# Local attention with its value product in banks of its own, and clipped attention issued two tiles at a time

## The chip, the cores and the metric

The kernel runs on one core of a Trainium2 chip. The metric is the device time of one execution in microseconds (us). Three timed runs of the kernel before took 2329.82, 2330.53 and 2332.7 us; their median is 2330.53 us. One further execution was profiled: it took 2336.06 us, of which the trace covers a span of 2334.3 us. All durations below are from that one.

## What is computed

The program is a chain of eight stages on 2048 tokens of width 128 (four attention layers and four feed-forward blocks), each with its own residual and normalisation. Two of them are touched.

The local stage has two layers. In each, queries and keys are normalised per head, turned by a rotary table, and a block of 64 queries attends to its own 64 keys and the 64 before:

```python
sim = einsum('bhwid,bhwjd->bhwij', bq, bk)       # 8 heads, 64 queries against 128 keys
mask = (i < j) | (i > j + WINDOW) | (j == -1)
sim = where(mask, -finfo.max, sim)
out = einsum('bhwij,bhwjd->bhwid', softmax(sim), bv)
x = x + out @ wo                                  # then layer norm, w1, a * gelu(g), w2, residual
```

The clipped stage is full attention over 512 tokens with 16 heads of 64, and relative positions clipped to 16 steps either way:

```python
sim = q @ k.T * scale + einsum('btd,tsd->bts', q, rel_k_table[idx]) * scale
attn = softmax(sim)
out = attn @ v + einsum('bts,tsd->btd', attn, rel_v_table[idx])
return out @ Wo.T + bo
```

## The kernel before, in words

Every stage is a class with a written list of steps (`order`), and one method for each engine (`on_tensor`, `on_vector`, `on_scalar`, `on_gpsimd`, `on_sync`). Each engine walks the same list and takes the steps that are its own, so the list sets the order on each engine. Nothing overtakes on an engine. Steps wait on each other by semaphores (`w.wait_ge`). Between stages, the last steps of one (`tail`) are dealt out among the first steps of the next (`head`).

PSUM has eight banks of 128x512 fp32. `Turns` deals banks to the steps named in its table: strictly in turn over the list, so with k banks a step gets the bank of the step k places before it among those steps. `freed` returns the semaphore that the new step must wait for, which is the one given by the step that empties the bank: for a projection `lin` that is `s_square`, since ScalarE squares the projection out of the bank after VectorE has read it.

**Local stage** (span about 207 to 640 us). 32 steps n (16 tiles of 128 tokens, two layers). Step n of the list works at several tiles at once, with p = n + 5: scores of tile n, projections `lin` of tile p for queries and keys (two matmuls of 128x128 by 512 columns, L1558), VectorE's rotary products on them (L1663 to L1665), ScalarE's squares (`square`, L1761), the transposes of two finished outputs (`ot`, L1602, emptied at L1788) and of the exponentials (`flip`, two of them, L1585, emptied at L1784), the value projection `v` of tile n + 2 (L1558 again, emptied at L1768), the transposes of queries and keys (`turnq`, `turnk`, L1564, emptied at L1776 and L1684), the exponential (L1779), the output product `out` (L1607), and the value product `av` of tile n - 1 (L1596; VectorE divides it at L1699 and L1702). TensorE's order in a step is: scores, lin, lin, ot, flip, v, flip, turnq, turnk, out, av. Steps of the feed-forward block (L1614 to L1632) are put in every four steps, between the second `flip` and `turnq` or at the end of the step.

Scores (L1573, the mask added by an identity matmul; L1578, the products, in quarters of 64x64) and `av` share banks 0 and 1, so the scores of n wait until VectorE has divided the `av` of n - 2 (`v_av`). The other nine bank users of a step (lin, lin, ot, flip, v, flip, turnq, turnk, out) take banks 2 to 7 in turn: six banks.

**Clipped stage** (about 1600 to 2220 us). 32 head pairs p (8 pairs in each of 4 batches), each of 4 tiles of 128 queries: 128 tiles n. A tile is: scores of two heads against 512 keys (L2323, banks 0 and 1 or 2 and 3), VectorE adds the relative part (L2405) and takes the maximum (L2408), ScalarE the exponential (L2488), eight transposes (L2330) through banks 4, 5 and 7 in turn, emptied by VectorE (L2414) and ScalarE (L2496), and the value product into bank 6 (L2345). GpSimd multiplies the band of near positions (L2534). Once for each head pair: the projections `q` and `k` (L2292), every second time `rel` (L2308), the sums of the band (`xsum`, `sums`: L2419, L2425), their transposes `wt` (L2352), and the matmul `close` (L2357) that ends the pair's bank 6. In some tiles there are value projections `vals` (L2288) and output products `wo` (L2362).

SyncE issues all transfers of that stage in list order from one queue: `lay` (L2551) stores the table of relative scores to memory, `skew` (L2555) loads it back at a slant, `band` (L2562) stores a tile's band, `gather` (L2567) loads its diagonal, `send` (L2572) stores one row of `wt`, and `rep` (L2577) loads it back to 64 partitions. Their waits are in `on_sync`. In the list before, `send` of a head pair stands in its fourth tile, then come `gather` in the next first tile and `rep` behind it, and `lay` stands in the second tile.

Of the kernel before, what the change touches and what calls it, by code (L numbers as in the profile page):

```python
# [41 lines left out]
def _tables():  # L42
    bf = np.dtype(mybir.dt.np(BF))
    f = np.float32
    c = {}
# [42 lines left out]
    b["loc"] = neg((x > i + 64) | (x < i))  # L88
    b["loc0"] = neg((x > i + 64) | (x < i) | ((p < 64) & (x < 64)))

# [1312 lines left out]
class Local:  # L1403
# [7 lines left out]
    def __init__(self, C):  # L1411
# [27 lines left out]
        for r in range(4):  # L1439
# [6 lines left out]
        self.early = Turns(self.plan[:self.head], 4, {"lin": S["s_square"]})  # L1446
        many = {step: (2, 3, 4) for step in self.plan[last:]}
        many.update({step: range(5) for step in self.plan[late:last]})
        self.ring = Turns(self.plan[self.head:], 6, {"lin": S["s_square"], "v": S["s_v"], "turnq": S["s_turnq"], "turnk": S["v_turnk"],
                                         "flip": S["s_flip"], "ot": S["s_ot"], "out": S["v_out"],  # L1450
                                         "two": S["v_two"], "hg": S["s_hg"], "ha": S["v_ha"], "four": S["v_four"], "five": S["s_five"],
                                         "turnx": S["s_turnx"]}, lambda step: many.get(step, range(6)))
        self.past = ((S["v_lin"], 31, 1), (S["t_lin"], 31, 1), (S["g_sum"], 31), (S["v_sum"], 31), (S["s_square"], 31, 1),
                     (S["s_turnx"], 0), (S["v_four"], 4), self.ring.held[5])
        C.met, C.left = last - late, [(S["v_av"], 31), self.ring.held[0], self.ring.held[1]]

    def order(self):
# [12 lines left out]
        for n in range(5):  # L1470
# [3 lines left out]
            if n == 3:  # L1474
                plan.extend([("v", 0), ("even", 0), ("v", 1), ("even", 1)])
        plan.extend([("scale", 0), ("turnq", 0), ("turnk", 0)])
        for n in range(N + 2):
            p = n + 5
            if n < N:
                plan.append(("scores", n))  # L1480
            if n + 1 < N:
# [27 lines left out]
            if 0 <= n - 1 < N:  # L1509
                plan.append(("av", n - 1))  # L1510
            if n >= 2 and n % 4 == 1:
                L, at = n // 4 - 1, 2 * n
                work += [(at, L, [("roll", L)]), (at + 2, L, [("ln", L)]), (at + 4, L, [("two", L)]),
                         (at + 5, L, [("hg", L, 0)]), (at + 6, L, [("ha", L, 0), ("hg", L, 1)]), (at + 7, L, [("ha", L, 1), ("hg", L, 2)]),
                         (at + 8, L, [("ha", L, 2)]), (at + 9, L, [("four", L)])]
                if L < NB:
                    work.append((at + 10, L, [("five", L)]))
                else:
                    work += [(at + 9, L, [("add", L), ("fin", L - NB)]), (at + 11, L, [("turnx", L - NB)])]
# [17 lines left out]
    def bank(self, step):  # L1537
        for turns in (self.early, self.ring):
            if step in turns.slot:
                return self.C.bank[2 + turns.slot[step]]  # L1540

    def on_tensor(self, e, w, step):
# [23 lines left out]
        elif kind == "scores":  # L1566
            QT, mask = self.QT[n % 2], W["loc0" if q == 0 else "loc"].unsqueeze(1).broadcast_to((128, 4, 128))
            w.wait_ge(S["v_soft"], n - 1)
            w.wait_ge(S["v_av"], n - 2)
            w.wait_ge(S["s_turnq"], n)  # L1570
            w.wait_ge(S["v_turnk"], n)
            for r in range(2):
                e.matmul(C.bank[r].rearrange("p (c j) -> p c j", c=4), W["idb"], mask, start=True, stop=False)  # L1573
            for c in range(4):
# [12 lines left out]
        elif kind == "av":  # L1587
            PT = self.PT[n % 2]
            w.wait_ge(S["v_soft"], n + 1)
            w.wait_ge(S["v_av"], n - 1)  # L1590
# [3 lines left out]
            for h in range(8):  # L1594
                for k, V in enumerate((self.VE, self.VO)):
                    i = e.matmul(C.bank[h // 4][64 * k:64 * k + 64, 65 * (h % 4):65 * (h % 4) + 65],  # L1596
                                 PT[:, 4 * (h % 2) + h // 2, 64 * k:64 * k + 64], V[n % 4][:, h, :], start=True, stop=True)
# [41 lines left out]
    def on_vector(self, e, w, step):  # L1639
# [55 lines left out]
        elif kind == "av":  # L1695
            va, r = S["v_av"], self.NM[n % 2][:, 8:16].rearrange("p (a h) -> p a h", a=2)
            s = C.PS[:, 0:2, 0:260].rearrange("p a (h c) -> p a h c", c=65)
            w.wait_ge(S["t_av"], n)
# [464 lines left out]
class Clipped:  # L2163
# [57 lines left out]
    def order(self):  # L2221
        plan, N = [("init",), ("turn",), ("q", 0), ("k", 0), ("table",), ("rel", 0), ("qr", 0), ("lay", 0), ("skew", 0)], 128
        plan.extend(("vals", 0, k, hf) for k in range(NT) for hf in range(2))
        for n in range(N + 10):
            p, q = n // 4, n % 4
            ahead = n < N and p + 1 < 32
            if ahead and q == 1:
                plan.extend([("qr", p + 1), ("lay", p + 1)])
            if n < N:
                plan.append(("scores", n))  # L2230
            if ahead and q == 0:
                if p % 2:
                    plan.append(("rel", (p + 1) // 2))
                plan.append(("q", p + 1))
            m = n - 32 - 3
            if m >= 0 and m % 32 < 4 and n < N:
                plan.append(("vals", m // 32 + 1, m % 32, 0))
            if 0 <= n - 2 < N:
                plan.append(("backv", n - 2, 0))
                plan.append(("backv" if (n - 2) % 4 == 3 else "backs", n - 2, 1))  # L2240
            if m >= 0 and m % 32 < 4 and n < N:
                plan.append(("vals", m // 32 + 1, m % 32, 1))
            if ahead and q == 0:
                plan.append(("k", p + 1))
            if n < N:
                plan.append(("exp", n))
            if 0 <= n - 1 < N:
                plan.append(("band", n - 1))
            if ahead and q == 2:
                plan.append(("skew", p + 1))  # L2250
            if q == 0 and 0 <= p - 1 < 32:
                plan.append(("gather", p - 1))
            if q == 0 and 0 <= p - 1 < 32:
                plan.append(("xsum", p - 1))
            if q == 2 and 0 <= p - 1 < 32:
                plan.append(("sums", p - 1))
            if 0 <= n - 6 < N:
                plan.append(("av", n - 6))
            if q == 3 and 0 <= p - 1 < 32:
                plan.extend([("wt", p - 1), ("send", p - 1)])  # L2260
            if q == 0 and 0 <= p - 2 < 32:
                plan.append(("rep", p - 2))
            if q == 1 and 0 <= p - 2 < 32:
                plan.append(("close", p - 2))
            b, m = (n - 38) // 32, (n - 38) % 32
            if 0 <= b < NB:
                if m < 2:
                    plan.extend([("wo", b, 2 * m), ("wo", b, 2 * m + 1)])
                if m == 1:
                    plan.append(("fin", b))  # L2270
                if m == 3:
                    plan.append(("turnx", b))
        return plan

# [722 lines left out]
```

## Time and profile before

| | |
|---|---|
| median of three timed runs | 2330.53 us |
| profiled execution, its span | 2336.06 us, 2334.3 us |
| TensorE busy with matmuls | 2077.1 us, 89% of the span |
| VectorE busy | 1532.0 us, 66% |
| ScalarE busy | 1145.4 us, 49% |
| GpSimd busy | 746.8 us, 32% |
| mean TensorE clock granted | 0.954 of full speed |
| transfers | 198.86 MB, mean 85 GB/s |

How to read it: the profile names engines PE (TensorE matmul), PEld (its weight load), DVE (VectorE), ACT (ScalarE), POOL (GpSimd) and SP (SyncE, which only issues transfers here). An instruction's duration begins when it starts and includes the time until its result is there, so durations of instructions that follow each other overlap, and the pitch of a group is better read from the start of one group to the start of the next. "Idle before" is the time in which an engine had nothing running, and what released it.

### The profile page before, as it was taken

Reading aid. Unit: us, or ns where it says so; the run is one execution under the profiler, and the core shown is the slowest. Engines: PE = TensorE matmul, PEld = TensorE weight load, DVE = VectorE, ACT = ScalarE, POOL = GpSimd, SP = SyncE. Lnnn points to the kernel's source line nnn. Section 1 sums busy time; section 2 is a strip of 40 time slices with the busy share of each in tenths; the row PEclk is TensorE's granted clock in tenths of the full one; section 3 lists DMA queues with packets and bytes.
Section 4 is the critical chain, followed back from the end, with each engine's and each line's share of the span. In section 5 each row is a group of like instructions: output and inputs, shape, how many; then the busy total and the mean of one; then the engine's idle time right before and its main releaser. Section 6 shows DMA issues by size and latency. Waiting matters only on the chain.

```text
span 2334.3 us, 40576 instructions
## 1 busy us (share of the span) xinstructions
PE 2077.1 (89%) x15640; PEld 1221.0 (52%) x15640; DVE 1532.0 (66%) x3079; ACT 1145.4 (49%) x1854; POOL 746.8 (32%) x1057
## 2 busy tenths in 40 slices
PE   5886789998868988999998988998999999999988
PEld 2332456666644454545564443445665656656546
DVE  5675677778678777746557772106776777767663
ACT  2565456556613545573333565224654655646432
POOL 4544433333127846450011320003223232232133
PEclk7998899999979999999998999999999999999999
DMA  4430111111323524202002310002563554535252
GB/s 142 127 92 2 28 29 28 31 27 29 95 77 123 153 72 133 82 3 100 1 4 89 100 47 33 0 0 100 173 193 103 182 160 138 167 114 182 82 111 55
DMA packets 183975, 198.86 MB, mean 85 GB/s; under 512 B 55922, under 2 KB 152486, under 8 KB 179302
## 3 DMA queue, kind: packets, MB, share of 16 engines
q1 hardware_dynamic: 183782, 196.27, 28.3%
q8 instruction: 123, 2.02, 0.4%
q14 instruction: 70, 0.57, 0.1%
HBM read 93.53 MB, written 92.08 MB: 80 GB/s over the span
## 4 chain that ended last, share of the span: by engine, by line
PE 45%; DVE 5%; ACT 2%; issue 1%; POOL 1%; DMA 1%; SPq 0%; DVEq 0%; ACTq 0%; POOLq 0%
PE PS L2323 6%; PE PS L2345 5%; PE PS L2330 5%; PE PS L2093 5%; PE PS L1946 3%; PE PS L2292 2%; PE PS L1933 2%; PE PS L1936 2%; PE PS L2357 1%; PE PS L2672 1%; PE PS L2362 1%; PE PS L597 1%; PE PS L2660 1%; PE PS L2662 1%; PE PS L2288 1%
## 5 line engine op out<-in xcount | busy, mean ns | idle before, releaser
L1275 ACT ACTIVATE AR<-PS 128x1024 f32<-128x1024 f32 x160 | 162.5, 1023 | 121.3 <-PE PS L1024 120.4
L718 ACT ACTIVATE AR<-PS 128x1024 f32<-128x1024 f32 x160 | 162.7, 1024 | 93.5 <-PE PS L576 46.3
L2488 ACT ACTIVATE AR<-PS,AR 128x512 f32<-128x512 f32 x256 | 173.5, 685 | 64.0 <-DVE AR L2408 63.8
L1128 DVE TENSOR_REDUCE AR<-PS 128x2 f32<-128x768 f32 (+1 forms) x192 | 160.0, 865 | 50.1 <-PE PS L1004 27.2
L2534 POOL TENSOR_TENSOR RA<-AR,RA 128x288 f32<-128x288 f32 x128 | 89.0, 695 | 235.4 <-ACT AR L2488 231.9
L2408 DVE TENSOR_REDUCE AR<-PS 128x2 f32<-128x1024 f32 x128 | 156.8, 1225 | 11.1 <-DVE PS L2405 0.5
L2323 PE MATMUL PS<-AR 64*128 64x200 f32 (+2 forms) x1280 | 148.0, 359 | 3.6 <-ACT AR L2488 3.6
L2330 PE MATMUL PS<-CC,AR 128*128 128x128 f32 x1024 | 138.5, 279 | 0.0
L2330 PEld LDWEIGHTS PS<-CC,AR 128*128 128x128 f32 x1024 | 113.6, 142 | 41.4 <-issue 37.7
L2323 PEld LDWEIGHTS PS<-AR 64*128 64x128 f32 x1280 | 103.9, 188 | 58.5 <-issue 50.7
L1817 POOL TENSOR_TENSOR AR<-AR 128x1024 f32<-128x1024 f32 x32 | 75.4, 2356 | 183.7 <-DVE AR L1665 183.7
L2405 DVE TENSOR_TENSOR PS<-PS,AR 128x288 f32<-128x288 f32 (+1 forms) x128 | 61.7, 482 | 91.1 <-PE PS L2323 80.6
L2093 PE MATMUL PS<-AR,RA 128*128 128x512 f32 x256 | 110.2, 593 | 0.0
L1558 PE MATMUL PS<-RA,AR 128*128 128x512 f32 x192 | 101.0, 638 | 10.2 <-ACT AR L1743 7.0
L597 PE MATMUL PS<-AR 128*32 128x512 f32 (+3 forms) x1024 | 103.0, 479 | 2.8 <-POOL AR L781 1.9
L554 PE MATMUL PS<-AR 48*128 48x512 bf16 (+7 forms) x512 | 70.1, 336 | 33.6 <-ACT AR L718 13.1
L658 DVE TENSOR_REDUCE AR<-PS 128x2 f32<-128x1024 f32 x64 | 77.6, 1223 | 21.6 <-PE PS L559 20.8
L1037 PE MATMUL PS<-AR 128*32 128x128 f32 (+3 forms) x1024 | 85.8, 441 | 4.3 <-POOL AR L1355 3.8
L1352 POOL TENSOR_SCALAR_AFFINE_SELECT AR<-AR 128x512 f32<-128x512 f32 (+1 forms) x128 | 72.2, 566 | 50.5 <-ACT AR L1275 50.2
L2029 ACT ACTIVATE AR<-PS 128x512 f32<-128x512 f32 x64 | 37.8, 597 | 101.4 <-PE PS L1933 98.0
L660 DVE TENSOR_REDUCE AR<-PS 128x2 f32<-128x768 f32 x64 | 61.3, 958 | 39.0 <-PE PS L559 38.7
L2093 PEld LDWEIGHTS PS<-AR,RA 128*128 128x128 f32 x256 | 48.7, 190 | 60.6 <-issue 60.6
(367 smaller groups left out, 5003.3 us busy)
## 6 DMA issues: line engine op xcount, KB each, us to landing
ZD<-RC SPq DMA_DIRECT2D x32, 1152.0 KB
AR<-ZD SPq DMA_DIRECT2D x32, 640.0 KB
ZP<-AR SPq DMA_DIRECT2D x128, 160.0 KB, 2.9
SP<-AR SPq DMA_DIRECT2D x40, 384.0 KB, 2.6
AR<-SP SPq DMA_DIRECT2D x128, 96.0 KB
RA<-SP SPq DMA_DIRECT2D x32, 384.0 KB
SP<-AR SPq DMA_DIRECT2D x40, 256.0 KB, 2.9
RC<-RC SPq DMA_DIRECT2D x64, 130.0 KB
```

What stands on the lines that cost most here:

```text
L597: i = e.matmul(b6[32 * j:32 * j + 32, 128 * kb:512], self.VP[b % 2][:, 16 * kb + 4 * (k % 4) + j, :], self.PT[at % 6][:, r, a:a + wd], sta ...
L718: e.activation(self.PT[m % 6], C.PS[:, 2 * s:2 * s + 2, :], ACT.Exp).then_inc(S["s_turned"].sem, 1)
L1128: i = e.tensor_reduce(nm[:, :, 4 * up + q:4 * up + q + 1], src[:, :, a:a + wd], AX, ALU.max, negate=True)
L1275: e.activation(self.PT[m % 6], C.PS[:, 2 * s:2 * s + 2, :], ACT.Exp).then_inc(S["s_turned"].sem, 1)
L1558: e.matmul(o, self.HT[:, L % NB, 64 + 128 * q:192 + 128 * q], W["wqkv" + str(L // NB)][:, 512 * x:512 * x + 512], start=True, stop=True).t ...
L2093: m = e.matmul(ba, w4[:, k, 128 * c:128 * c + 128], src[:, k, :], start=k == 0, stop=k == 3)
L2323: i = e.matmul(C.bank[2 * (n % 2) + hh][:, lo:hi], self.QT[p % 2][h, 128 * q:128 * q + 128], src[p % 2][h, lo:hi], start=True, stop=True)
L2330: i = e.transpose(o[:, 128 * k:128 * k + 128], self.PP[n % 5][:, hh, 16 + 128 * k:144 + 128 * k], C.ident)
L2345: i = e.matmul(C.bank[6][64 * hh:64 * hh + 64, 128 * lo:128 * hi].rearrange("p (a c) -> p a c", a=hi - lo), V[:, k, 64 * h:64 * h + 64], p ...
L2408: e.tensor_reduce(self.NMX[n % 4], s, AX, ALU.max, negate=True).then_inc(S["v_scores"].sem, 1)
L2488: i = e.activation(self.PP[n % 5][:, hh, 16:528], C.bank[2 * (n % 2) + hh], ACT.Exp, bias=self.NMX[n % 4][:, hh:hh + 1], accum_out=self.DE ...
L2534: e.tensor_tensor(self.XM[:, 2 * q:2 * q + 2, :], self.PP[n % 5][:, :, 128 * q:128 * q + 144], W["edge"].unsqueeze(1).broadcast_to((128, 2 ...
```

## The change

In the local stage, `av` gets banks 2 and 3 for itself, the scores keep 0 and 1, and the other nine bank users of a step share banks 4 to 7: four banks in turn instead of six. `scores` of n + 1 stands right behind `av` of n - 1 in the list, ahead of the sums and of the feed-forward steps of that place, and no longer waits for `v_av`; `av` no longer waits for `v_soft`. The mask is added by four matmuls with a 64x64 identity instead of two with a 128x128 one. In the last steps three banks are dealt instead of five.

```diff
-        self.ring = Turns(self.plan[self.head:], 6, {"lin": S["s_square"], "v": S["s_v"], ...
+        self.ring = Turns(self.plan[self.head:], 4, {"lin": S["s_square"], "v": S["s_v"], ...
...
-                                         "turnx": S["s_turnx"]}, lambda step: many.get(step, range(6)))
+                                         "turnx": S["s_turnx"]}, lambda step: range(3 if step in few else 4))
...
+        plan.append(("scores", 0))
         for n in range(N + 2):
             p = n + 5
-            if n < N:
-                plan.append(("scores", n))
...
             if 0 <= n - 1 < N:
                 plan.append(("av", n - 1))
+            if n + 1 < N:
+                plan.append(("scores", n + 1))
...
             w.wait_ge(S["v_soft"], n - 1)
-            w.wait_ge(S["v_av"], n - 2)
...
-            for r in range(2):
-                e.matmul(C.bank[r].rearrange("p (c j) -> p c j", c=4), W["idb"], mask, start=True, stop=False)
+            for k in range(2):
+                for r in range(2):
+                    h = slice(64 * r, 64 * r + 64)
+                    mask = W["loc" if q or k else "loc0"][h].unsqueeze(1).broadcast_to((64, 4, 128))
+                    e.matmul(C.bank[r][64 * k:64 * k + 64, :].rearrange("p (c j) -> p c j", c=4), W["idb"][h, 64 * r:64 * r + 64],
+                             mask, start=True, stop=False)
...
             PT = self.PT[n % 2]
-            w.wait_ge(S["v_soft"], n + 1)
...
-                    i = e.matmul(C.bank[h // 4][64 * k:64 * k + 64, 65 * (h % 4):65 * (h % 4) + 65],
+                    i = e.matmul(C.bank[2 + h // 4][64 * k:64 * k + 64, 65 * (h % 4):65 * (h % 4) + 65],
```

In the clipped stage the list is written anew in pairs of tiles. What each step does is unchanged. The new body, for n = 0, 2, 4, ... with p = n // 4, and `first` for the first pair of a head pair:

```diff
+        for n in range(0, N + 12, 2):
+            p, first = n // 4, n % 4 == 0
+            ahead = n < N and p + 1 < 32
+            if first:
+                if 0 <= p - 2 < 32:
+                    plan.append(("rep", p - 2))
+                if ahead:
+                    plan.extend([("qr", p + 1), ("lay", p + 1)])
+                if 0 <= p - 1 < 32:
+                    plan.append(("gather", p - 1))
+            else:
+                if ahead:
+                    plan.append(("skew", p + 1))
+                if 0 <= p - 1 < 32:
+                    plan.append(("sums", p - 1))
             if n < N:
+                plan.extend([("scores", n), ("scores", n + 1)])
+            plan.extend(("av", m) for m in (n - 6, n - 5) if 0 <= m < N)
+            for m in (n, n + 1):
+                if m < N:
+                    plan.append(("exp", m))
+                if 0 <= m - 2 < N:
+                    plan.extend([("backv", m - 2, 0), ("backv" if (m - 2) % 4 == 3 else "backs", m - 2, 1)])
+                if m < N:
+                    plan.append(("band", m))
+            if first:
+                if ahead:
+                    plan.extend([("q", p + 1), ("k", p + 1)])
+                if 0 <= p - 1 < 32:
+                    plan.append(("xsum", p - 1))
+            else:
+                if ahead and p % 2 == 0 and p + 2 < 32:
+                    plan.append(("rel", p // 2 + 1))
+                if 0 <= p - 1 < 32:
+                    plan.extend([("wt", p - 1), ("send", p - 1)])
...
+            if first and 0 <= p - 2 < 32:
+                plan.append(("close", p - 2))
```

The value projections now stand four in a row at the end of a pair, the output products two in a row.

## Rows read from the trace of the kernel before

**Rows 1.** The page's costliest groups: busy, mean ns of one, idle before.

```profile
L2488 ACT ACTIVATE AR<-PS,AR 128x512 f32<-128x512 f32 x256 | 173.5, 685 | 64.0 <-DVE AR L2408 63.8
...
L2408 DVE TENSOR_REDUCE AR<-PS 128x2 f32<-128x1024 f32 x128 | 156.8, 1225 | 11.1 <-DVE PS L2405 0.5
```

**Rows 2.** TensorE in time order, one plain local step: start, busy, group [idle before].

```profile
300.74 0.60 PE L1573 MATMUL PS<-CB 128*128 128x512 bf16 x2 [1.04 <-DVE RC L1702]
...
301.28 1.10 PE L1578 MATMUL PS<-AR 64*64 64x128 f32 x32
...
302.31 1.99 PE L1558 MATMUL PS<-RA,AR 128*128 128x512 f32 x4
...
305.01 1.03 PE L1558 MATMUL PS<-RA,AR 128*128 128x512 f32 x2
...
305.87 0.60 PE L1585 MATMUL PS<-CC,AR 128*128 128x128 f32 x4
...
306.46 0.66 PE L1564 MATMUL PS<-CC,AR 128*128 128x128 f32 x4
...
307.44 0.66 PE L1564 MATMUL PS<-CC,AR 128*128 128x128 f32 x4 [0.32 <-ACT AR L1761]
...
308.92 1.15 PE L1596 MATMUL PS<-RC,AR 128*64 128x65 f32 x32
...
311.11 0.60 PE L1573 MATMUL PS<-CB 128*128 128x512 bf16 x2 [1.04 <-DVE RC L1702]
```

**Rows 3.** ScalarE in time order, the same step.

```profile
305.80 0.60 ACT L1761 ACTIVATE AR<-PS 128x512 f32<-128x512 f32 x1
306.28 0.62 ACT L1768 ACTIVATE RC<-PS 128x512 f32<-128x512 f32 x1
...
306.76 0.63 ACT L1761 ACTIVATE AR<-PS 128x512 f32<-128x512 f32 x1
```

**Rows 4.** TensorE, starts of the mask matmuls of two later local steps.

```profile
434.70 0.61 PE L1573 MATMUL PS<-CB 128*128 128x512 bf16 x2 [0.46 <-DVE RC L1702]
...
572.08 0.99 PE L1573 MATMUL PS<-CB 128*128 128x512 bf16 x2 [3.50 <-DVE RC L1702]
```

**Rows 5.** ScalarE, the first square in the local step with the normalisations.

```profile
428.83 0.60 ACT L1761 ACTIVATE AR<-PS 128x512 f32<-128x512 f32 x1 [1.19 <-DVE AR L1665]
```

**Rows 6.** TensorE, the key transposes of the same step.

```profile
430.75 0.65 PE L1564 MATMUL PS<-CC,AR 128*128 128x128 f32 x4 [0.61 <-ACT AR L1761]
```

**Rows 7.** Stretches: length, busy (count) of PE, PEld, DVE, ACT, POOL, clock, DMA.

```profile
381.00:383.00 2.00, 2.00 (x12) 1.78 (x12) 1.85 (x3) 1.97 (x3) 2.00 (x2) 0.51 0.57 130
```

**Rows 8.** TensorE in time order, clipped stage: one tile, and two matmuls that end head pairs.

```profile
1862.49 1.13 PE L2357 MATMUL PS<-AR,RA 128*128 128x512 f32 x2
1863.55 1.16 PE L2323 MATMUL PS<-AR 64*128 64x200 f32 x12
1864.63 1.09 PE L2330 MATMUL PS<-CC,AR 128*128 128x128 f32 x8
1865.65 1.08 PE L2345 MATMUL PS<-RA,AR 128*64 128x128 f32 x8
1866.67 1.14 PE L2323 MATMUL PS<-AR 64*128 64x256 f32 x8
...
1879.39 1.13 PE L2357 MATMUL PS<-AR,RA 128*128 128x512 f32 x2
```

**Rows 9.** SyncE's queue, clipped stage: start and duration of the issue.

```profile
1860.82 0.45 SPq L2551 DMA_DIRECT2D ZD<-RC  x1
...
1866.20 0.36 SPq L2555 DMA_DIRECT2D AR<-ZD  x1
```

**Rows 10.** Transfers issued in 1861.2 to 1862 (right behind a `lay`): KB, us to landing.

```profile
ZP<-AR SPq DMA_DIRECT2D x1, 160.0 KB, 4.9
```

**Rows 11.** Transfers issued in 1855.5 to 1857 (the queue otherwise empty).

```profile
ZP<-AR SPq DMA_DIRECT2D x1, 160.0 KB, 1.9
```

More of the change, by code:

```diff
@@ L88, in _tables @@
     b["loc"] = neg((x > i + 64) | (x < i))
-    b["loc0"] = neg((x > i + 64) | (x < i) | ((p < 64) & (x < 64)))
+    b["loc0"] = neg((x > i + 64) | (x < i) | (x < 64))
     slopes = ((2.0 ** (-8.0 / 16)) ** np.arange(1, 17, dtype=np.float64)).astype(f)
@@ L1446, in __init__ @@
         self.early = Turns(self.plan[:self.head], 4, {"lin": S["s_square"]})
-        many = {step: (2, 3, 4) for step in self.plan[last:]}
-        many.update({step: range(5) for step in self.plan[late:last]})
-        self.ring = Turns(self.plan[self.head:], 6, {"lin": S["s_square"], "v": S["s_v"], "turnq": S["s_turnq"], "turnk": S["v_turnk"],
+        few = set(self.plan[late:])
+        self.ring = Turns(self.plan[self.head:], 4, {"lin": S["s_square"], "v": S["s_v"], "turnq": S["s_turnq"], "turnk": S["v_turnk"],
                                          "flip": S["s_flip"], "ot": S["s_ot"], "out": S["v_out"],
                                          "two": S["v_two"], "hg": S["s_hg"], "ha": S["v_ha"], "four": S["v_four"], "five": S["s_five"],
-                                         "turnx": S["s_turnx"]}, lambda step: many.get(step, range(6)))
+                                         "turnx": S["s_turnx"]}, lambda step: range(3 if step in few else 4))
         self.past = ((S["v_lin"], 31, 1), (S["t_lin"], 31, 1), (S["g_sum"], 31), (S["v_sum"], 31), (S["s_square"], 31, 1),
-                     (S["s_turnx"], 0), (S["v_four"], 4), self.ring.held[5])
-        C.met, C.left = last - late, [(S["v_av"], 31), self.ring.held[0], self.ring.held[1]]
+                     (S["s_turnx"], 0), (S["v_four"], 4), self.ring.held[3])
+        C.met, C.left = last - late, [(S["v_soft"], 31), (S["v_av"], 31)]
     def order(self):
@@ L1537, in bank @@
     def bank(self, step):
-        for turns in (self.early, self.ring):
+        for turns, first in ((self.early, 2), (self.ring, 4)):
             if step in turns.slot:
-                return self.C.bank[2 + turns.slot[step]]
+                return self.C.bank[first + turns.slot[step]]
     def on_tensor(self, e, w, step):
@@ L1566, in on_tensor @@
         elif kind == "scores":
-            QT, mask = self.QT[n % 2], W["loc0" if q == 0 else "loc"].unsqueeze(1).broadcast_to((128, 4, 128))
+            QT = self.QT[n % 2]
             w.wait_ge(S["v_soft"], n - 1)
-            w.wait_ge(S["v_av"], n - 2)
             w.wait_ge(S["s_turnq"], n)
             w.wait_ge(S["v_turnk"], n)
-            for r in range(2):
-                e.matmul(C.bank[r].rearrange("p (c j) -> p c j", c=4), W["idb"], mask, start=True, stop=False)
+            for k in range(2):
[4 more added lines that the diff above has]
+                             mask, start=True, stop=False)
             for c in range(4):
@@ L1696, in on_vector @@
             va, r = S["v_av"], self.NM[n % 2][:, 8:16].rearrange("p (a h) -> p a h", a=2)
[L1697 removed]
+            s = C.PS[:, 2:4, 0:260].rearrange("p a (h c) -> p a h c", c=65)
             w.wait_ge(S["t_av"], n)
@@ L2223, in order @@
         plan.extend(("vals", 0, k, hf) for k in range(NT) for hf in range(2))
-        for n in range(N + 10):
-            p, q = n // 4, n % 4
+        for n in range(0, N + 12, 2):
+            p, first = n // 4, n % 4 == 0
             ahead = n < N and p + 1 < 32
-            if ahead and q == 1:
-                plan.extend([("qr", p + 1), ("lay", p + 1)])
-            if n < N:
[L2230 to L2264, printed above, removed]
@@ L2265, in order @@
+            m = n - 32
+            if m >= 0 and m % 32 in (2, 4) and n < N:
+                plan.extend(("vals", m // 32 + 1, m % 32 - 2 + i, hf) for i in range(2) for hf in range(2))
             b, m = (n - 38) // 32, (n - 38) % 32
             if 0 <= b < NB:
-                if m < 2:
-                    plan.extend([("wo", b, 2 * m), ("wo", b, 2 * m + 1)])
-                if m == 1:
+                if m < 4:
+                    plan.extend([("wo", b, m), ("wo", b, m + 1)])
+                if m == 2:
@@ L2270, in order @@
                     plan.append(("fin", b))
-                if m == 3:
+                if m == 4:
                     plan.append(("turnx", b))
+            if first and 0 <= p - 2 < 32:
+                plan.append(("close", p - 2))
         return plan
```

## The prediction

> **What bounds the kernel now.** I read the page first, then the two touched stages by stretches, then their instructions in time order. TensorE carries the chain that ended last. In the clipped stage it never rests in the steady stretches; VectorE comes second, with 1.225 us for each maximum [rows 1]. So a wait that is put into TensorE's queue is paid in full in either stage, unless one of the same length goes. In the local stage the reader is to see in [rows 2] which waits TensorE has in a step, and that some are waits for a bank.
>
> A plain local step, without feed-forward work, takes 311.11 - 300.74 = 10.37 us [rows 2]. Pitches: a 512-column fp32 projection 0.86 us (305.01 to 305.87), so the `av` group, whose 65-column products come to about the same, is issued by 308.92 + 0.87 = 309.79. The next mask starts at 311.11: 1.32 us are lost because VectorE must first divide the `av` that lies in the scores' banks. Two smaller waits stand before the transposes: `turnq` could go at 306.30 and goes at 306.46, `turnk` could go at 306.89 and goes at 307.44, each right behind the end of a square: 305.80 + 0.60 = 306.40 and 306.76 + 0.63 = 307.39 [rows 2, 3]. These are bank waits of the six-bank ring: 0.71 us together.
>
> **The local stage, part by part.** *Mask in quarters.* The two full mask matmuls take 301.28 - 300.74 = 0.54 us [rows 2]. Four quarters on four different parts of the array should run side by side, as the scores' own quarters do (32 of 128 columns in 1.03 us, a quarter of what they would take in a row). I take 0.21 us off a step; bounds 0 (they queue) and 0.33.
>
> *Own banks for `av`.* The 1.32 us go in plain steps. In the steps whose feed-forward group has only transposes at the end the wait shows as 0.46 us idle, about 0.65 us with what drains before it, in the first row of [rows 4]; the steps with a hidden-layer matmul in that place show none, so nothing is won there.
>
> *Four banks instead of six.* This is the term that decides. Nine users a step, dealt strictly in turn: `v` is four places behind the first `lin`, the second `flip` four behind the second `lin`. With six banks it was `turnq` and `turnk` that stood on those banks, three and four matmul groups later. Now `v` waits for the first square. Taking the first `lin` as zero (302.31), the square starts at 3.49 and ends at 4.09; that time does not move, since VectorE's rotary products and ScalarE's two earlier copies are where they were. `v` was at 2.70 (305.01) and goes at 4.16: 1.46 us idle. Then ScalarE's order bites: `v` is copied out before the second square. `v` is issued by 5.02, its copy starts 0.27 later (the lag of the other copies behind their matmuls) at 5.29, the second square 0.48 behind it (306.28 to 306.76) at 5.77, ends at 6.39, and the second `flip`, which needs that bank, goes at 6.43 instead of 3.56 (305.87): 2.87 us late [rows 2, 3]. Nothing on TensorE can fill that, because it issues in order.
> For all steps with projections (n = 0 to 26) this is new. `turnq` and `turnk` then stand on banks that are long free, so their 0.71 us go.
>
> By kind of step: plain (n = 2 to 6), +2.87 - 0.71 - 1.32 - 0.21 = +0.63 us. The later ones come in fours, five of each kind. With hidden-layer matmuls (two kinds), +2.87 - 0.21, about +2.6. With the block's last product and the transposes of the next layer's input: the next projections wait for a chain that begins with `av` and ends with ScalarE's copy of that input, so neither mask nor bank helps, +2.87. With the normalisations, VectorE is late anyway: the first square ends at 429.43 [rows 5], and TensorE's transposes already waited for both squares, the key transposes until 430.75 [rows 6]. Now `v` (0.86), lag 0.27, its copy 0.48, the square 0.60 and 0.06 come one behind the other after 429.49: `flip` at 431.76, `turnk` 0.87 later at 432.63, 1.87 late; less 0.65, 0.21 and some 0.2 of changed shapes, +0.8. Sum: 5 x (0.63 + 2.6 + 2.6 + 2.87 + 0.8) = +47.5 us. The first two steps wait for VectorE and GpSimd at half clock; between 0 and +5.8, I take +2, nearer to the end at which the other wait covers it. The steps after the last projection have no squares and win what they waited for `v_av`: 3.50 us in one, the last row of [rows 4], and a like wait five steps on, but VectorE, which was late, stays late, and three banks for five cost something: between -9 and +4, I take -4. **Local: +45 us**, from +30 to +60.
>
> **The clipped stage.** *Fewer changes of shape.* A tile takes 1866.67 - 1863.54 = 3.13 us in three groups of 1.09, 1.02 and 1.02 us. Each group's columns fill 0.85 us (a projection's 512 columns take 0.86 [rows 2], and each group has as many once two halves run side by side), so 0.57 us of a tile goes in three changes between groups [rows 8]. Pairs halve it: 4 x 0.285 = 1.14 us for each head pair. `close` behind `k` and `wt` behind transposes save some 0.5 us more: 1.65 us in all, of 1879.39 - 1862.49 = 16.90 us (with `rel`; without it the same matmuls are 16.0 us apart). Over 32 head pairs that is -53 us, the lower bound.
>
> *What the pair puts in its place.* VectorE now takes two tiles' scores (2 x about 1.72 us: the addition and its 1.225 us maximum [rows 1]) before it copies transposes, so it is busy from 1.2 to 4.7 us after the pair's first matmul. The fourth group of transposes needs the bank of the first (three banks), and waits for that copy: I work it out as 0.35 us in the first pair and 0.55 us in the second, where VectorE starts 0.2 us late because `close` and `sums` are in front. That leaves 16.0 - 15.3 = 0.7 us a head pair, -23 us.
>
> *SyncE's queue.* `send` now comes at the very end of a head pair (ScalarE reaches `wt` some 1.3 us into the next), and right behind it stands `rep`, which waits until `send` has landed, then `lay`, then `gather`. A lone 160 KB store lands in 1.9 us [rows 11]; a 2 KB one in as much or a little less. So `rep` is issued at about 3.2, `lay` at 4.5 to 5.1, `gather` half a microsecond later, all counted from the pair's first matmul. Behind a `lay` a store took 4.9 us instead of 1.9 [rows 10], so `gather` lands at 9.9 to 10.5. VectorE's `sums` waits for it, and behind `sums` in VectorE's queue are the scores of the second pair, then everything. Without the transfer `sums` would start at 9.5. So 0.4 to 1.0 us are lost again a head pair. `skew` must wait for `lay`, 1866.20 - 1860.82 = 5.4 us [rows 9], and then has some 6 us until its data are needed; it just fits.
> Taken together: 15.7 to 16.3 us against 16.0 before. I take -0.15 us x 32 = -5 us. The rows of value projections, four in a row, lose waits of some 3 us in each of three batches, and a final normalisation now holds up a whole pair's scores, about 2 us in each of four: -9 + 8, about -1, and some -2 for `close` in the ends. **Clipped: -8 us**, from -53 to +25.
> The Trainium skill, in "DMA: Bandwidth & Descriptors", section "Queues, rings and completion order", says that one engine's transfers are spread over rings, that each ring starts its descriptors in order, but that completion is not first-in first-out for an issuing engine. By that a small `gather` might land ahead of the large `lay`, and the clipped stage would keep its -23 us. The 4.9 us of [rows 10] speak for the other reading here.
>
> **Sum.** 45 - 8 = +37 us, on the profiled execution's own 2336.1 us: 2373. The median of the timed runs lies 5.5 us below that execution, so I say 2330.5 + 37 = **2368 us**.
>
> **Rivals.**
> *The clock falls in the new waits.* In one of the steps with normalisations, after two gaps of TensorE close together, the granted clock was 0.51 for some 3 us [rows 7], half speed; two such groups then took about 1.7 us more. The others of that kind did not fall. The new order has two gaps of 1.3 to 1.4 us in every step. Against it: there is a 0.86 us projection between them and each is no longer than the mask wait of the plain steps, at full clock. If half to all of 27 steps fall, +23 to +46: about 2400. 0.12.
> *`gather` comes later still*, by a slow `rep` (its issue lasts up to 1.2 us each of two): `sums` at 11, each head pair 0.8 us over before, +25 in place of -8: 2330.5 + 45 + 25 = 2400. 0.10.
> *The pairs win more than the banks lose.* If transfers land ahead of `sums` and VectorE keeps up, the clipped stage gives its whole -53, with -3 at value projections; local +45: 2330.5 - 11 = 2320. It decides from the point where `sums` never waits and the fourth transposes find their bank free. For it speaks that VectorE is busy only some 13 of 16 us; against it the counted 4.7 us. 0.10.
> *The four banks do not bind*, because a square comes early enough: then local gives only -0.21 x 27 - 1.32 x 5 - 0.65 x 10 - 4, about -23, and with clipped -8 it is 2300. [Rows 2, 3] speak flatly against it: the two transposes wait on just these squares today. 0.05.
> A mixture that ends within 0.2% of before: 0.05.
>
> **How the numbers follow.** My forecast has 0.58, with its own range 2345 to 2385. Less than 0.2% (4.7 us) cannot be told from no change. Faster: 0.10 + 0.05 = 0.15; same 0.05; slower 0.58 + 0.12 + 0.10 = 0.80. The range that leaves out 2 in 10 goes from 2320 to 2405.
>
> **What would show it.** In the local stage: `v` (L1558) idle before, released by ScalarE L1761, about 1.4 us, and the second `flip` (L1585) the same, in each step up to n = 26; no wait of L1573 for L1702; plain steps near 11.0 us. In the clipped stage: `close` 15.7 to 16.3 us apart without `rel`; L2425 waiting for RA<-ZP; L2330 waiting for L2414. Wrong would be: `v` at 2.7 us behind `lin`, or L2425 never waiting, or mean clock well under 0.95.

## The result, and the profile after

The changed kernel takes 2377.52 us (median of four runs, 2373.6 to 2378.56); the kernel before took 2331.61 us in the runs beside it. The ratio is 1.0192, 95% interval 1.0174 to 1.0209: 46 us slower. 2368 us had been forecast, with 2320 to 2405 as the range. The execution profiled took 2378.22 us, its span 2376.5 us, 42.2 us more than the span of before; the profiled execution of before (2336.06 us) is 4.5 us above its median, hence the difference between 46 and 42.

The first part of the page of the changed kernel: TensorE has fewer busy microseconds than before, in a longer span, so the time is in waits. The last line is TensorE's granted clock in tenths, in 40 slices of the span.

```profile
PE 2043.5 (86%) x15704; PEld 1238.9 (52%) x15704; DVE 1537.4 (65%) x3079; ACT 1142.2 (48%) x1854; POOL 744.8 (31%) x1057
...
PEclk7998889999987999898999899999999999999999
```

A plain step of the local stage, TensorE in time order, is the answer to [rows 2]. The columns are start, busy, group and the idle time before it with its releaser (L1575 is the mask, L1581 the scores, L1588 `flip`, L1598 `av`, L1763 the square).

```profile
303.05 0.41 PE L1575 MATMUL PS<-CB 64*64 64x512 bf16 x4
...
304.26 1.99 PE L1558 MATMUL PS<-RA,AR 128*128 128x512 f32 x4
...
308.41 1.12 PE L1558 MATMUL PS<-RA,AR 128*128 128x512 f32 x2 [1.29 <-ACT AR L1763]
...
310.79 0.66 PE L1588 MATMUL PS<-CC,AR 128*128 128x128 f32 x4 [1.26 <-ACT AR L1763]
...
314.23 0.41 PE L1575 MATMUL PS<-CB 64*64 64x512 bf16 x4
```

The reader is to see both waits that were forecast, in the forecast places, each released by the square; and that the next mask has no wait before it. Counted from the first `lin` (304.26), `v` starts at 4.15 us, where 4.16 were forecast, and the second `flip` at 6.53 us, where 6.43 were. This step takes 11.18 us where 10.37 were before. The step ahead of it took 12.70 and so did the one behind: every second plain step has something more. A stretch of two microseconds in the next step, in the view by windows of the changed kernel, shows what it is: the granted clock, 0.50 (columns as in [rows 7]):

```profile
322.00:324.00 2.00, 2.00 (x10) 2.00 (x11) 0.00 (x0) 0.60 (x1) 0.00 (x0) 0.50 0.50 106
```

In the clipped stage TensorE's order is as written, and the answers to [rows 8] are these: two head pairs end 16.58 us (with `rel`) and 14.97 us (without) apart, where 16.90 and 16.0 were before, and the fourth group of transposes waits for VectorE's copy in the pairs in which VectorE was late.

```profile
1916.57 1.02 PE L2358 MATMUL PS<-AR,RA 128*128 128x512 f32 x2
1917.52 2.04 PE L2324 MATMUL PS<-AR 64*128 64x200 f32 x20
1919.48 1.95 PE L2346 MATMUL PS<-RA,AR 128*64 128x128 f32 x16
1921.36 1.53 PE L2331 MATMUL PS<-CC,AR 128*128 128x128 f32 x12
1923.59 0.66 PE L2331 MATMUL PS<-CC,AR 128*128 128x128 f32 x4 [0.70 <-DVE AR L2415]
...
1933.15 1.02 PE L2358 MATMUL PS<-AR,RA 128*128 128x512 f32 x2
1934.10 2.04 PE L2324 MATMUL PS<-AR 64*128 64x200 f32 x20
...
1939.94 0.60 PE L2353 MATMUL PS<-CC,RA 128*128 128x128 f32 x4
...
1948.12 1.02 PE L2358 MATMUL PS<-AR,RA 128*128 128x512 f32 x2
```

Where the 42.2 us of span are: the last `out` product of the local stage starts at 697.18 us, 56.8 us later than before (640.39). The first `close` of the clipped stage is 60.1 us late (1704.72 against 1644.60), so the stages between added 3. From the first to the last `close` pass 546.35 us where 565.77 passed: 19.4 us less. The end adds 1.5.

Differences of a few microseconds in the time of a whole kernel need care here. The stages between the two changed ones have the same code in all kernels but for the hand-over at both ends, yet from the last `out` to the first `close` pass 1004.2 us in the kernel before, 1007.5 in the changed one and 1016.8 in the longest below. The mean granted clock of that stretch is 0.96 in the first and 0.94 to 0.95 in the long ones; the differences come in jumps all along the stretch, not at its ends. So the experiments are also read stage by stage.

### The profile page after: what moved, and what is told of

It reads as the page before. It is cut to its first block, busy times and chain, and to the rows that moved or that the text cites. A ratio compares the mean times of both kernels' runs of the same rounds, so it can differ in the third digit from the quotient of the medians.

```text
span 2376.5 us, 40686 instructions
## 1 busy us (share of the span) xinstructions
PE 2043.5 (86%) x15704; PEld 1238.9 (52%) x15704; DVE 1537.4 (65%) x3079; ACT 1142.2 (48%) x1854; POOL 744.8 (31%) x1057
## 4 chain that ended last, share of the span: by engine, by line
PE 30%; DVE 9%; DMA 5%; ACT 5%; issue 2%; SPq 2%; POOL 0%; DVEq 0%; ACTq 0%; POOLq 0%
PE PS L2095 5%; DMA RA<-ZP 4%; DVE AR L2409 3%; PE PS L1948 3%; PE PS L1935 2%; PE PS L1938 2%; ACT AR L2489 2%; PE PS L2324 2%; PE PS L2673 1%; PE PS L2331 1%; PE PS L597 1%; PE PS L2363 1%; PE PS L2346 1%; PE PS L2661 1%; PE PS L2663 1%
## 5 line engine op out<-in xcount | busy, mean ns | idle before, releaser
L1819 POOL TENSOR_TENSOR AR<-AR 128x1024 f32<-128x1024 f32 x32 | 75.1, 2346 | 219.5 <-DVE AR L1667 219.5
L2324 PE MATMUL PS<-AR 64*128 64x200 f32 (+2 forms) x1280 | 132.5, 351 | 3.0 <-ACT AR L2489 3.0
L1824 POOL TENSOR_TENSOR AR<-AR 128x1024 f32<-128x1024 f32 x32 | 60.8, 1902 | 69.8 <-DVE AR L1681 69.8
```

The lines of the kernel that those rows point to most:

```text
L2324: i = e.matmul(C.bank[2 * (n % 2) + hh][:, lo:hi], self.QT[p % 2][h, 128 * q:128 * q + 128], src[p % 2][h, lo:hi], start=True, stop=True)
```

## The experiments

All are compared with runs of the kernel before made beside them. Times are medians.

**The two parts alone.** Each keeps one of the two classes as changed and the other as before:

```diff
-class Clipped: (changed)        x1_local_only
+class Clipped: (as before)
...
-class Local: (changed)          x2_clipped_only
+class Local: (as before)
```

> The new local stage with the clipped stage of before. Theory: the local stage with four banks dealt in turn loses 57 to 60 us (the first `close` of the clipped stage came 60 us later in the changed kernel), so about 2331 + 59 = 2390 us, some 13 above the changed kernel. Rival (the loss is in a hand-over between stages or in the clipped stage's start): at most +45, 2376 us or less.

Measured 2399.34 us, ratio 1.0293 (1.0276 to 1.0310), +68 us.

> The paired clipped stage with the local stage of before. Theory: its first to last `close` takes 19 us less, so about 2312 us, and the two parts add up to the whole. Rival (the gain of the clipped stage needs the shifted state of the changed kernel, or transfers order it another way): -8 us or less, 2323 us or more.

Measured 2311.95 us, ratio 0.9926 (0.9910 to 0.9943), -19.4 us. The paired clipped stage is worth as much without the new local stage: from first to last `close` pass 543.39 us here, 22.4 less than before, against 19.4 less in the changed kernel. The local stage alone costs some 9 us more than expected; together they give +49, the changed kernel +46. The excess is not in the local stage itself, whose last `out` starts at 697.66 us, 57.3 us late, as in the changed kernel. The stages between took 1009.1 us, 4.9 more than before, and the clipped stage as long as before (565.8 us). The other 6 are mostly the profiled execution of before, which lies 4.7 us above the median of before in the runs beside these (2331.38 us).

**Four banks, dealt in halves.**

```diff
-     "turnx": S["s_turnx"]}, lambda step: range(3 if step in few else 4))
+     "turnx": S["s_turnx"]}, lambda step: range(3) if step in few else (0, 1) if step[0] in ("lin", "turnq", "turnk") else (2, 3))
```

> The changed kernel, with the local stage's four banks dealt in two halves: projections and the transposes of queries and keys take two, everything else the other two. `v` then waits for the copy of `ot`, not for a square. Theory (the bank behind the square is the loss): `v` goes some 0.5 us after its place of before and the second `flip` without a wait, about 2.4 us less in each of 27 steps, and the clock's falls go too: 2377 - 65 - 10, about 2300 us. Rival (four banks are too few however they are dealt): 2350 us or more. Rival (half the loss is the clock, which falls anyway): about 2312.

Measured 2310.75 us, ratio 0.9920 (0.9904 to 0.9937): 67 us under the changed kernel. `v` now waits for the copy of `ot` (L1790) and the square holds up only the key transposes, as in [rows 2] (TensorE in time order, x3_split_banks):

```profile
295.20 1.13 PE L1558 MATMUL PS<-RA,AR 128*128 128x512 f32 x2 [0.31 <-ACT AR L1790]
296.17 0.60 PE L1588 MATMUL PS<-CC,AR 128*128 128x128 f32 x4
296.60 0.60 PE L1564 MATMUL PS<-CC,AR 128*128 128x128 f32 x4
297.58 0.65 PE L1564 MATMUL PS<-CC,AR 128*128 128x128 f32 x4 [0.39 <-ACT AR L1763]
```

So the number of banks was not the loss; which step stood behind which was. A plain step takes 9.33 us. The whole lies 11 us above the expected 2300, and the later steps show where: four of them take 49.2 to 49.7 us, mask to mask, hardly less than the 48.9 to 50.2 of before. The last `out` starts at 631.04 us, 9 us earlier than before.

**The second square ahead of `v`,** banks as changed:

```diff
-            if n + 2 < N:
-                plan.extend([("v", n + 2), ("even", n + 2)])
             if p < N:
                 plan.append(("square", p, 1))
+            if n + 2 < N:
+                plan.extend([("v", n + 2), ("even", n + 2)])
```

> The changed kernel, with one line of the local list moved: the second square ahead of `v`, so ScalarE does it before it copies the value projection. Theory (serial chain v, its copy, square, flip): the first wait of 1.3 us stays, the second of 1.26 us before the second `flip` goes, but for some 0.1: 27 x 1.3 = 35 us, and the clock stays up, 10 more: about 2335 us. Rival (the wait just moves on to the next transposes, which need ScalarE's copies): 2365 us or more.

Measured 2321.86 us, ratio 0.9959 (0.9947 to 0.9971): 56 us less than the changed kernel, where 45 at most were expected. The first wait stays as it was and the second is gone (TensorE in time order, x4_square_first):

```profile
295.32 1.13 PE L1558 MATMUL PS<-RA,AR 128*128 128x512 f32 x2 [1.29 <-ACT AR L1763]
296.28 0.60 PE L1588 MATMUL PS<-CC,AR 128*128 128x128 f32 x4
296.72 1.04 PE L1564 MATMUL PS<-CC,AR 128*128 128x128 f32 x8
```

One ScalarE copy that stood in front of the square was half of the waits. From the first mask to the last `out` the stage takes 396.7 us, where the changed kernel took 449.5: 52.8 less. The 1.26 us in 27 steps make 34 of them; the other 19 fit what the next run puts down to the clock. The remaining 3 us lie outside the stage.

**Work in the waits.** Ahead of `v`, and of the second `flip`, in nearly all steps with projections (49 matmuls in all):

```diff
+        if kind == "v" and 4 <= n and n + 3 < 32 or kind == "flip" and key[1] == 1 and 2 <= n and n + 6 < 32:
+            m = n if kind == "v" else n + 3
+            w.wait_ge(S["v_av"], m - 4)
+            e.matmul(C.bank[2], self.HT[:, 0, 64:192], W["wqkv0"][:, 0:512], start=True, stop=True)
```

> The changed kernel with a matmul of 128x128 by 512 fp32 columns put into each of the two waits of a local step (before `v` and before the second `flip`), written into a bank that the next value product overwrites; 0.86 us of work in waits of 1.4 us. Theory (the part of the local loss beyond the counted waits is the clock falling in them): no stretch of the local steps at half clock but at its start and end, 10 to 15 us less, 2364 us. Rival (the clock plays no part, the extra is elsewhere): within 3 us of the changed kernel, or slower.

Measured 2354.14 us, ratio 1.0091 (1.0073 to 1.0109): 23 us less than the changed kernel, by adding work; 10 to 15 had been expected. The added matmuls cost nothing: a plain step takes 11.18 us, as the steps of the changed kernel at full clock do. The last `out` starts at 673.15 us instead of 697.18, 24 us earlier. In the same stretches of the view by windows, first this kernel and then the changed one:

```profile
274.00:278.00 4.00, 4.00 (x57) 2.68 (x54) 3.25 (x7) 1.18 (x3) 0.22 (x1) 1.00 0.02 4
296.00:300.00 4.00, 4.00 (x69) 2.67 (x64) 2.94 (x5) 1.08 (x2) 0.00 (x0) 1.00 0.00 0
...
458.00:464.00 6.00, 6.00 (x89) 4.59 (x88) 3.56 (x6) 4.80 (x5) 0.31 (x1) 1.00 0.11 25
```

```profile
274.00:278.00 4.00, 3.92 (x20) 3.81 (x20) 0.69 (x1) 2.46 (x5) 0.00 (x0) 0.58 0.29 67
296.00:300.00 4.00, 2.74 (x11) 1.92 (x11) 1.76 (x2) 1.68 (x3) 3.69 (x2) 0.73 0.28 66
...
458.00:464.00 6.00, 4.74 (x19) 3.56 (x18) 3.29 (x4) 3.16 (x5) 4.21 (x2) 0.52 0.19 44
```

The stage did not begin at the same moment in each kernel (first mask at 248.22 us before, 247.68 changed, 244.48 here), so it is measured from the first mask to the last `out`: 392.2 us before, 428.7 here, 449.5 in the changed kernel. The new order costs it twice: 36.5 us with the waits filled, and 20.8 us more by what the clock did in and after them. The mean granted clock from 255 us to the last `out` is 0.97, 0.99 and 0.93 in the three; the stage of before has a few falls of its own, so against a stage without any the waits cost somewhat more than 36.5 us.

**`gather` first in SyncE's list,** ahead of `rep` and `lay`:

```diff
             if first:
+                if 0 <= p - 1 < 32:
+                    plan.append(("gather", p - 1))
                 if 0 <= p - 2 < 32:
                     plan.append(("rep", p - 2))
...
-                if 0 <= p - 1 < 32:
-                    plan.append(("gather", p - 1))
```

> The changed kernel with `gather` ahead of `rep` and `lay` in SyncE's list. Theory (VectorE's `sums` waits for a gather that lies behind the large store): the 11 us of waits for RA<-ZP go and 5 to 11 us with them, 2368 us. Rival (the wait is covered by the fourth transposes' wait for VectorE, or `rep` and `skew` come late in its place): within 2 us of the changed kernel.

Measured 2371.96 us, ratio 1.0168 (1.0148 to 1.0187): 5.6 us less, which the two intervals alone would not tell from noise. In the changed kernel, the view of waits from 1680 to 2180 us (engine, line, releaser: us in total, times, longest):

```profile
DVE RA L2426 <- DMA RA<-ZP: 11.1, 15, 2.7
```

That group is gone with `gather` in front, and with it most of TensorE's wait for the copy that frees the bank of the fourth transposes. The waits from the first to the last `close`, first in the changed kernel and then with `gather` first:

```profile
PE PS L2331 <- DVE AR L2415: 14.7, 18, 2.7
...
PE PS L2331 <- DVE RA L2415: 3.0, 6, 1.1
```

```profile
PE PS L2331 <- DVE AR L2415: 5.4, 6, 0.9
...
PE PS L2331 <- DVE RA L2415: 1.0, 2, 0.6
```

The stage itself gains 12.0 us (534.3 instead of 546.35 between these `close`), so more than the whole kernel: the stages between took 1015.8 us here, 8.2 more than in the changed kernel. The worst case shows the chain, VectorE and then TensorE in time order in the changed kernel: VectorE's `sums` 2.73 us late, then the fourth transposes, then half clock for the scores (3.14 us instead of 2.04). That head pair took 20.05 us.

```profile
1886.10 0.42 DVE L2426 TENSOR_REDUCE RA<-RA 128x8 f32<-128x256 f32 x1 [2.73 <-DMA RA<-ZP]
```

```profile
1890.56 0.66 PE L2331 MATMUL PS<-CC,AR 128*128 128x128 f32 x4 [2.69 <-DVE AR L2415]
...
1893.00 3.14 PE L2324 MATMUL PS<-AR 64*128 64x256 f32 x20
```

**The mask in quarters alone,** on the kernel before (the two changed pieces of code as in the diff, nothing else):

> The kernel before with only the mask in quarters. Theory: 0.2 to 0.3 us less in each of 32 steps where TensorE sets the pace, 7 to 9 us less: 2323 us. Rival (the scores' end, not the mask, waits, or the quarters run one behind the other): no difference, 2331 us.

Measured 2328.91 us, ratio 0.9985 (0.9972 to 0.9998), -4.8 us. The forecast price is right in the local stage: its last `out` starts 9.3 us earlier (631.06 against 640.39), 8.1 of them after the first mask. The profiled spans differ by 8.5 us: the stages between took 4.3 us longer and the clipped stage 3.2 us less, with the same code in both kernels. The rest of the way to 4.8 is which execution was profiled: that of before lies 2.4 us above the median of before in the runs beside these (2333.67 us), the other 1.4 below its own.

**All together, and once without own banks.** Three kernels: both local edits (halved banks, square first); the same with `gather` first; and as third the local stage of before with its six banks, with quarters and square first, beside the paired clipped stage with `gather` first.

> The same without the `gather` edit. Theory: 5 us above the one with it, about 2301 us. Rival (with another local stage `sums` never waits for `gather`): equal to it.

Measured 2311.61 us, ratio 0.9904 (0.9884 to 0.9925).

> The changed kernel with the three edits together: banks dealt in halves, the second square ahead of `v`, `gather` ahead of `rep` and `lay`. Theory (each takes away another wait): of the halved banks' kernel (2311 us) there remain a wait of 0.3 us before `v` and one of 0.4 us before the key transposes in each of 27 steps; the second goes, 10 us, and `gather` brings 5: 2296 us. Rival (VectorE, with some 7.8 us of work in a plain step of 9.3, now sets the pace): 2306 us or more.

Measured 2305.41 us, ratio 0.9875 (0.9854 to 0.9897). That is 9 us above the expected 2296 and near the rival's 2306, but not for the rival's reason: a plain step fell to 8.72 us, and TensorE waits in it for ScalarE alone (0.31 us). Four later steps take 49.4 us, no less than with halved banks alone.

> The local stage of before (value product in the scores' banks, six banks for the rest) with the mask in quarters and the second square ahead of `v`, and the paired clipped stage with `gather` first. Theory (banks of its own for `av` are worth 1.3 us in plain steps and 0.65 in two of four later ones, some 15 us, once the other four are dealt well): about 10 to 15 us above the kernel with all three edits, 2308 us. Rival (own banks are worth nothing beside VectorE's pace): equal to it or below.

Measured **2295.8 us**, ratio 0.9839 (0.9816 to 0.9862): the fastest of all, 37.6 us under the kernel before and 82 under the changed one. `gather` first is worth 6 us between the first two of the three, and 8.3 us in the clipped stage itself (534.3 against 542.7 us between first and last `close`). But here I was wrong about the own banks: the kernel without them is 10 us faster than the one with them, not slower. A cycle of four steps in each, TensorE in time order at the masks (the first, the second and the fifth; first the kernel with own banks, y7_all, then y10_six_banks_best):

```profile
472.22 0.41 PE L1575 MATMUL PS<-CB 64*64 64x512 bf16 x4
...
482.86 0.41 PE L1575 MATMUL PS<-CB 64*64 64x512 bf16 x4
...
521.64 0.41 PE L1575 MATMUL PS<-CB 64*64 64x512 bf16 x4
```

```profile
473.97 0.41 PE L1576 MATMUL PS<-CB 64*64 64x512 bf16 x4 [0.45 <-DVE RC L1706]
...
485.15 0.41 PE L1576 MATMUL PS<-CB 64*64 64x512 bf16 x4
...
521.73 0.41 PE L1576 MATMUL PS<-CB 64*64 64x512 bf16 x4 [0.45 <-DVE RC L1706]
```

Four such steps take 49.42 us with own banks and 47.76 with six shared ones. Plain steps are the other way round, 8.72 against 9.69. So the own banks win in the plain steps and lose in the later ones. Over the whole local stage they lose 5.3 us (last `out` at 631.33 against 625.99 us). Of the 12.6 us between the two profiled spans, 9.4 lie in the stages between, whose code is the same in both but for the hand-overs (1016.8 against 1007.5 us). So only about half of the 10 us can be put down to the local stage. Two things eat the gain in the later steps. With own banks, two banks serve the `lin` and the rotary transposes and two all the rest, and each step waits for them (y7_all):

```profile
402.14 1.13 PE L1558 MATMUL PS<-RA,AR 128*128 128x512 f32 x2 [0.31 <-ACT RC L1790]
404.10 2.94 PE L1634 MATMUL PS<-RA,AR 128*128 128x128 f32 x24 [0.40 <-ACT RC L1770]
413.42 1.99 PE L1558 MATMUL PS<-RA,AR 128*128 128x512 f32 x4 [1.73 <-ACT AR L1745]
```

And the scores stand ahead of the feed-forward steps, so the transposes of the next layer's input are a scores group later, and the projections wait 1.73 us for ScalarE's copy of it, against 1.21 with the order of before (y10_six_banks_best):

```profile
415.55 1.99 PE L1558 MATMUL PS<-RA,AR 128*128 128x512 f32 x4 [1.21 <-ACT AR L1747]
```

## Why the prediction was right, and where not

*The whole: the right way and near, in part by luck.* The median went up by 46 us where +37 had been forecast. The local stage was forecast 12 us too low (+45, measured +57), the clipped stage 11 us too high (-8, measured -19.4); the two errors all but cancel.

*The bank behind the square: right, place and size.* 1.46 us idle were forecast before `v` and about 1.4 before the second `flip`; the profile shows 1.29 and 1.26, since it counts a matmul to its modelled end, and the two start within 0.1 us of the forecast places. The halved banks took the loss away with the same number of banks, and the square ahead of `v` took exactly the second wait.

*Sum of the local stage: right in sign, too small, by errors that partly cancel.* Forecast +45, measured +57 (x1_local_only and the last `out`). With the waits filled and the clock up (x5_filler), only 36.5 are left of the 45. A plain step loses 0.81 us there (11.18 against 10.37), 0.63 was forecast. Over-counted were two others. The first two steps take 18.61 us, mask to mask, where 21.53 were: 3 less, where 2 more had been taken. TensorE there waited 1.70 us before `av` and 1.04 us before the mask, and has neither wait now (0.22 us for the copy of the keys is left); part of the 3 is the clock, too. A cycle of four later steps takes 56.71 us where before took 48.93 to 50.22: 6.5 to 7.8 more, where 2.6 + 2.6 + 2.87 + 0.8 = 8.9 had been forecast, so 5 to 12 us too much over the five.

What was left out of the sum is the clock. It stood among the rivals with 0.12 and +23 to +46 us; it came true near its lower end, +21, together with the forecast. Two steps of the argument against it failed. One was a reading of the trace before: of the five steps with normalisations not one but three fell to half clock, and they show in the step times (14.08, 14.43 and 14.45 us, against 13.16 in the other two). The other was that each wait is no longer than the mask wait of the plain steps, which ran at full clock. That compared one gap at a time; two of them with one projection between went with a fall in every second plain step. Waits and clock should have been one case, not a forecast and a rival.

*Own banks for `av`: the wait went, as forecast.* No L1575 waits for `av` any more between 270 and 620 us. That it was worth little stood in the prediction (1.32 us in five steps, 0.65 in ten); that the later steps, with four banks for the rest and the scores in their new place, give it all back was not foreseen.

*Quarters: right, a little more than forecast.* 0.21 us a step were taken, 0.33 at most. x8_quarters_only shows 0.36 in a plain step (10.01 against 10.37), 0.98 in a cycle of four at full clock (47.95 against 48.93), 8.1 us over the stage. The quarters also have the scores' own shape, so a change of shape may go too; no run separates that.

*The clipped stage: right in sign, too small: -19.4 against -8.* Three terms were mis-sized, two of them against each other.

The gain from fewer changes of shape was put at 1.65 us a head pair, and is 1.0. Steady pairs in which TensorE never waits take 14.97 us, against 16.01 before; with `rel` it is 16.58 - 0.70 = 15.88 against 16.90. The three groups of two tiles (scores, value products, transposes) take 5.84 us (1934.10 to 1939.94), where twice one tile took 6.24, so pairing saves 0.4 us of the 0.57 that had been taken, and 0.3 in the other pair.

What the pairs pay back was put at 0.9 us a head pair for the fourth transposes and 0.4 to 1.0 for the queue, some 48 us in all; TensorE's waits for the fourth transposes are 17.7 us (rows above), of which 6.4 remain with `gather` first. The mechanism is as forecast, its price about a third. The two errors nearly cancel: outside the batch ends the stage wins 0.3 us a head pair, where 0.15 had been forecast.

The batch ends were put at -3 us together and give most of the gain. The three stretches that hold them (four head pairs each) take 81.32, 81.08 and 81.00 us after and 86.25, 84.64 and 86.24 before, 13.7 us less in all. Some 3 of these are half clock that before had in two of the three. The forecast waits came as said: the 3.1 us before `vals` are gone in each, and 2.0 us behind the final normalisation are new. What was missed is the gain from fewer changes of shape: TensorE's work without its waits takes some 5 us less a stretch, 1.2 us a head pair, and the fourth transposes take back 2.5 to 2.7 of them, not nearly all.

*The queue.* The forecast put `gather`'s landing at 9.9 to 10.5 us after the pair's start and `sums`' own time at 9.5. Where `sums` had to wait, it started 9.6 to 10.6 us after the pair's first matmul (once 12.2), and in steady pairs where not, from 9.4. It was late in 15 head pairs of some 28, mostly by under 1 us. The reading of the Trainium skill by which a small transfer may overtake a large one ("DMA: Bandwidth & Descriptors", "Queues, rings and completion order") is not what this case shows: each time that `sums` waited, `skew`, which is issued only when `lay` has landed, had been issued 0.5 us or more before it, so `gather` landed behind `lay`; ahead of it it was on time.

## What to carry to other kernels

When banks are dealt in turn, write down for each step whose bank it gets and when that bank is emptied. Going from six to four moved the slowest-emptied bank from the last step of the round to one in its middle, and dealing the same four in two halves gave all of it back. A wait before TensorE has to be priced with the clock that it may cost afterwards: here two waits of 1.3 us a step cost 21 us in clock over the stage, beside their own length. A buffer given to one user is taken from the others: here the kernel with own banks was 1 us faster in the steps that had little else to do and 0.4 us slower in the many that had much; part of the 0.4 is the place of the scores in the list, which no run separates from the banks. And a change is best measured in its own stage: the stages between, whose own code is untouched, moved by up to 12.6 us.

## What the hardware showed that was not expected

Adding 49 matmuls of 0.86 us made the kernel 23 us faster, since, but for two short falls, the granted clock stayed at its upper level (2.4 GHz) where it had fallen to the lower (1.2 GHz, 0.50) during the second of two gaps of 1.3 us with one projection between them (at 274.0, 297.9 and 321.7 us).

No simple rule of gaps comes out of these runs. With one gap of 1.29 us a step (x4_square_first) the clock stayed up in all steps from 324 to 572 us. With gaps of 0.3 to 0.4 us (x3_split_banks) it fell in two places between 260 and 560, and both stand behind a single longer one, the 1.74 us wait for the next layer's input. And in the kernel before, the same two gaps of 1.29 and 0.60 us stand before the transposes of three steps with normalisations, at 379.3, 429.5 and 478.4 us: the clock fell behind the first and the third, not behind the second.
